# Routing the second experts batch by batch, and starting their blocks among the attention's last steps

## What is computed

```python
x = x + attn0(layernorm(x))                 # linear attention, width 64
x = x + ffn0(layernorm(x))                  # 8 experts, top 2, and a shared expert
x = x + attn1(layernorm(x))                 # 16 heads, window of 128 keys on each side
x = x + ffn1(layernorm(x))                  # 8 experts, top 1

def ffn1(x, W1, W2, Wg, bg):                # W1 (8, 256, 1024), W2 (8, 1024, 256)
    xf = x.reshape(4096, 256)
    one_hot = jax.nn.one_hot(jnp.argmax(xf @ Wg + bg, axis=-1), 8)
    h = jax.nn.gelu(jnp.einsum('td,edh->eth', xf, W1), approximate=True)
    return jnp.einsum('etd,te->td', jnp.einsum('eth,ehd->etd', h, W2), one_hot)
```

## Time and profile before

| | |
|---|---|
| median of 3 runs | 1568.0 us (1565.64 to 1570.33) |
| the profiled execution | 1571.8 us, its span 1568.9 us |
| TensorE busy | 1431.9 us, 91% of the span |
| VectorE, GpSimd, ScalarE busy | 740.2, 450.8, 449.9 us |
| mean granted TensorE clock | 0.954 of 2.4 GHz |
| bytes moved by DMA | 139.78 MB |

### The profile page before, as it was taken

The page is one execution under the profiler, slowest core; times in us unless marked ns, Lnnn a source line. Parts: engine busy times, 40 slices in busy tenths (PEclk is TensorE's granted clock), DMA queues, the critical chain, the costliest instruction groups (busy, mean ns, idle before and its releaser), DMA issues.

```text
span 1568.9 us, 23779 instructions
## 1 busy us (share of the span) xinstructions
PE 1431.9 (91%) x7707; PEld 1037.5 (66%) x7707; DVE 740.2 (47%) x2386; ACT 449.9 (29%) x763; POOL 450.8 (29%) x533
## 2 busy tenths in 40 slices
PE   7999999899999999897988989889887569999998
PEld 4666655567777776455555656666655359999997
DVE  5643347333333333336677777777662342222221
ACT  1211211011111121113455555565544111111121
POOL 1100000143222220603345354453222023443443
PEclk9998999999999999998899999999988779999999
DMA  9300100011122111134335354553430941111111
GB/s 336 102 28 27 41 0 1 14 51 61 61 64 63 63 62 44 57 97 143 90 110 164 120 149 119 154 157 100 120 105 15 338 162 51 51 55 49 50 56 32
DMA packets 88356, 139.78 MB, mean 89 GB/s; under 512 B 10637, under 2 KB 52751, under 8 KB 88240
## 3 DMA queue, kind: packets, MB, share of 16 engines
q1 hardware_dynamic: 72832, 104.02, 21.1%
q0 software_dynamic: 12096, 32.13, 7.1%
q10 hardware_dynamic: 3312, 2.12, 0.5%
HBM read 86.46 MB, written 52.17 MB: 88 GB/s over the span
## 4 chain that ended last, share of the span: by engine, by line
PE 76%; DVE 9%; DMA 6%; issue 4%; ACT 3%; POOL 1%; ACTq 1%; DVEq 0%; SPq 0%; POOLq 0%
PE psum L663 11%; PE psum L544 9%; PE psum L845 8%; PE psum L867 7%; PE psum L642 6%; PE psum L555 5%; PE psum L734 5%; PE psum L689 3%; DMA qT<-max_T 3%; PE psum L711 3%; DVE work L1519 2%; PE psum L471 2%; PE psum L790 2%; ACT arena L1045 2%; PE psum L461 2%
## 5 line engine op out<-in xcount | busy, mean ns | idle before, releaser
L1519 DVE CUSTOM_DVE_ANT_0 work<-psum,mask 128x384 bf16<-128x384 f32 (+1 forms) x512 | 229.7, 487 | 122.4 <-PE psum L689 119.4
L1045 ACT ACTIVATE arena<-psum 128x512 f32<-128x512 f32 (+1 forms) x256 | 179.5, 703 | 182.4 <-PE psum L711 172.9
L1626 POOL DMA_INDIRECT work<-normed,token_of x110 | 104.4, 949 | 395.7 <-PE psum L624 211.3
L663 PE MATMUL psum<-arena,work 128*128 x568 | 187.5, 473 | 2.8 <-ACT work L961 2.4
L689 PE MATMUL psum<-kz,qT 96*128 96x384 f32 (+1 forms) x512 | 170.2, 413 | 7.8 <-DVE small L1519 7.0
L711 PE MATMUL psum<-qT,kz 100*128 100x384 f32 (+1 forms) x512 | 131.5, 337 | 31.1 <-ACT arena L1045 16.8
L544 PE MATMUL psum<-arena 128*128 128x512 f32 x320 | 152.1, 621 | 0.0
L845 PE MATMUL psum<-work,X 128*128 128x128 f32 x1248 | 146.9, 276 | 0.0
L845 PEld LDWEIGHTS psum<-work,X 128*128 128x128 f32 x1248 | 143.8, 193 | 0.1
L689 PEld LDWEIGHTS psum<-kz,qT 96*128 96x128 f32 x512 | 91.1, 199 | 76.9 <-issue 38.9
L867 PE MATMUL psum<-arena,work 128*128 x624 | 141.0, 379 | 0.0
(11 more groups left out here) (170 smaller groups left out, 1987.7 us busy)
## 6 DMA issues: line engine op xcount, KB each, us to landing
strips<-hi SPq DMA_DIRECT2D x64, 256.0 KB
arena<-in_w SPq DMA_DIRECT2D x16, 1024.0 KB, 12.6
kz<-strips SPq DMA_DIRECT2D x64, 192.0 KB, 3.2
qT<-strips SPq DMA_DIRECT2D x32, 384.0 KB, 4.9
results<-work SPq DMA_DIRECT2D x71, 128.0 KB, 1.7
strips<-lo SPq DMA_DIRECT2D x32, 256.0 KB
normed<-work SPq DMA_DIRECT2D x15, 512.0 KB, 5.1
X<-in_x SPq DMA_DIRECT2D x8, 512.0 KB, 9.5
```

Source lines behind the costliest of these rows:

```text
L663: m = e.matmul(psum[:, pair[u], 0:INTER], xsT0[:, b % 2, c * P:(c + 1) * P], wu0[:, bass.ds(x, 1), c, u * INTER:(u + 1) * INTER], start=(c ...
L1045: e.activation(pT[:, j, 2 * half:2 * half + 2, 0:w], src, ACT.Exp, scale=1.0 / E ** 0.5).then_inc(p_exped, 1)
L1519: e.tensor_tensor_reduce(masked[:, n % 2, 0:w], psum[:, bank_of["scores", u, i, hd], at:at + w], mask[:, P - off:P - off + w], 1.0, MASKED ...
L1626: e.indirect_dma_start(out=xs[:, b % 3, :], out_offset=None, in_=normed[l], in_offset=bass.IndirectOffsetOnAxis(ap=token_of[:, l, b:b + 1] ...
```

## The change

Routing by batch. The gate of batch b comes at step 46 instead of 50. Then `dve_pick` (step 47) finds each token's expert, `pe_ranks` (48) counts with 8 small products each token's rank among all tokens of its expert so far, `dve_slots` (49) makes its place, and `pool_place` (50) writes the token numbers with four indirect transfers into a table in DRAM, in which each expert has 32 rows of 128 places. The table is filled with a padding number at step -12.

Two lists. After batch 4 (step 113) and after batch 7 (step 161) `dve_list` works out which rows of the table hold blocks, `pool_list` gathers them, `pe_list` and `dve_tokens` turn them into lists of tokens. The first list has the full blocks of the first five batches, 12 of them; the second has the other 27.

Blocks in the loop. `ROWS_AT`, `UP_AT` and `DOWN_AT` say in which step a block's transposes, first and second product stand: the 12 early ones from step 128 to 166, among the attention's last steps, the others one every two steps from 168. `FETCH_AT` says when its rows are gathered.

Weights. `sp_weights` loads the block's own w1 and w2 (1 MB each) from DRAM for every block, into two buffers each; the array in DRAM is laid out so that a partition's part is one run of 8 KB. VectorE's copies of w1 are gone, and so are TensorE's reads of the expert's number. The first products of all blocks now use PSUM banks 0 and 1, the transposes bank 2, the second products the ring of 6 and 7.

Batch 6's two stores to DRAM move from SyncE to ScalarE.

```diff
-TURN_AT, GATE_AT = (-11, 43), 50
+TURN_AT, GATE_AT = (-11, 43), 46
+EARLY_B = 5
+EARLY = (EARLY_B * N - NX * (P - 1)) // P
+LISTED_AT = (PRE * (EARLY_B - 1) + 49, PRE * (B - 1) + 49)
+ROWS_AT = [128, 129, 131, 133, 135, 137, 139, 141, 144, 149, 153, 159]
+UP_AT = ROWS_AT[1:] + [162]
+DOWN_AT = [132, 134, 136, 138, 140, 142, 145, 150, 154, 160, 163, 166]
+LATE_AT = LISTED_AT[1] + 7
+ROWS_AT += [LATE_AT - 1] + [LATE_AT + 2 * k for k in range(NBLK1 - EARLY - 1)]
+UP_AT += [LATE_AT + 2 * k for k in range(NBLK1 - EARLY)]
+DOWN_AT += [LATE_AT + 2 * k + 3 for k in range(NBLK1 - EARLY)]
+FETCH_AT = [122, 123, 124] + [at - 4 for at in ROWS_AT[3:EARLY]]
+FETCH_AT += [max(at - 4, LISTED_AT[1] + 5) for at in ROWS_AT[EARLY:]]
...
+            m = e.matmul(psum[:, bk, 0:n], before[:, :], flat, start=True, stop=False, skip_group_check=True)
+            for d in range(1, TPB):
+                m = e.matmul(psum[:, bk, d * w:n], ones[:, :], flat[:, 0:n - d * w], start=False, stop=False,
+                             skip_group_check=True)
+            e.wait_ge(so_far_made, b + 1)
+            for t in range(TPB):
+                m = e.matmul(psum[:, bk, t * w:(t + 1) * w], ones[:, :], so_far, start=False, stop=True,
+                             skip_group_check=True)
...
+        def pe_up1(e, k):
+
+            e.wait_ge(xsT_made[1], k + 1)
+            e.wait_ge(w1_got[k % 2], 16 * (k // 2 + 1))
+            for u in range(2):
+                fill(e, ("up1", k, u), u)
...
+                for k in blocks_at(s, ROWS_AT, 1):
+                    act_turned_rows(e, 1, k, xsT1)
+                for k in blocks_at(s, UP_AT, 1):
+                    act_hidden1(e, k)
                 for u, j in unit(s, 7, 4):
                     act_exp(e, u, j, 0)
...
-                        if (norm, b, i) == (3, B - 1, 1):
+                        if norm == 3 and b >= B - 2 and i == 1:
                             keep_residual(e, b)
                             keep_normed(e, 1, b)
...
                 for b, _ in batch(s, GATE_AT + 1):
-                    dve_gate(e, 1, b)
+                    dve_pick(e, b)
+                for b, _ in batch(s, GATE_AT + 3):
+                    dve_slots(e, b)
+                for i in range(2):
+                    if s == LISTED_AT[i]:
+                        dve_list(e, i)
...
+                for b, _ in batch(s, GATE_AT + 4):
+                    pool_place(e, b)
+                for i in range(2):
+                    if s == LISTED_AT[i] + 2:
+                        pool_list(e, i)
+                for k in blocks_at(s, FETCH_AT):
+                    pool_rows1(e, k)
+                for k in blocks_at(s, UP_AT):
+                    pool_residual1(e, k)
+                for k in blocks_at(s, DOWN_AT, 2):
+                    pool_out(e, k)
...
+            for t in range(b * TPB, (b + 1) * TPB):
+                e.indirect_dma_start(out=slots, out_offset=bass.IndirectOffsetOnAxis(ap=slot_of[:, 2, t:t + 1], axis=0),
+                                     in_=token_no[:, t:t + 1], in_offset=None).then_inc(placed, 16)
...
+            if k == 0:
+                e.wait_ge(*done["again", NU - 4, TPB - 1, G - 1])
+            if k == 1:
+                e.wait_ge(*done["again", NU - 3, TPB - 1, G - 1])
+                e.wait_ge(*done["again", NU - 2, TPB - 1, G - 1])
+            if k >= 2:
+                e.wait_ge(*done["up1", k - 2, 1])
+            x = e.value_load(blk_expert[0:1, 1, k:k + 1], min_val=0, max_val=NX - 1)
+            e.dma_start(w1_now[k % 2].rearrange("p c n -> p (c n)"),
+                        a["w1"][bass.ds(x, 1), :, :].rearrange("x p n -> p (x n)")).then_inc(w1_got[k % 2], 16)
+            if k >= 2:
+                e.wait_ge(*done["down1", k - 2])
+            e.dma_start(w2_now[k % 2].rearrange("p c n -> p (c n)"),
+                        a["w2"][bass.ds(x, 1), :, :].rearrange("x p n -> p (x n)")).then_inc(w2_got[k % 2], 16)
...
+            for k in range(NBLK1):
+                sp_weights(e, k)
```

580 lines of the change are left out of this document (322 added, 258 removed).

## The result

The changed kernel takes 1694.6 us (median of 4 runs, 1690.0 to 1698.8), the kernel before 1566.8 beside it: a ratio of **1.082** (95% interval 1.077 to 1.086). The prediction said 1559, in a range of 1538 to 1578. The profiled execution has a span of 1688.1 us, 119.2 more than the 1568.9 of before. Every further kernel was timed beside runs of its own of the kernel before, whose medians lie between 1561.1 and 1567.1 us; so a difference between two medians can hold up to 6 us that are not the edit's, and the ratios are the safer measure.

A forecast was written before the change was run, and what follows sets the result against it. TensorE was taken as the bound, its stretch from 1188 to 1282 us as the target. Terms -60 + 19.4 + 6.7 + 15 + 10 = -8.9 us took the 1568.0 median to 1559, range 1538 to 1578.

The forecast's parts named there:

- Routing taken out of the gap: Stretch from last maxima to late blocks: waits, low clock and routing work, plus row waits, could go; ceiling 60 us.
- Picks and ranks: Attention, batches 0 to 4: new TensorE products 10.4 us plus 9 us behind VectorE, 19.4 us slower.
- The gate moves from step 50 to 46, same work: nothing by itself.: Attention, each batch's gate: standing four steps earlier is the same work and costs 0 us.
- GpSimd's four scatters ... nothing.: Attention, each batch: four issues of 1.31 us ahead of the next mask, which has about 8 us to spare; cost 0.
- Waits from step 128 on: Early blocks among the attention's last steps: remaining TensorE waits and low clock cost 15 us, bounds 9 and 25.
- (4) of "What would show it": ScalarE behind step 128: seven table loads of 1.28 us, with exponentials' waits next to them.
- The stream: 27 late blocks: loading weights for every block adds 0.37 us a block, 10 us in all.
- L: Late blocks: time from a second product's end until two 1 MB weight transfers land; 7.7 to 8.7 us, 8.2 taken.
- the rival: Late blocks' first products waiting for w1: weight loading becomes the bound, L 9.5 us, kernel 1576 us; chance 0.18.
- sign (5): Late blocks' weight transfers: w1 lands near 6 us.
- its rivals: Late blocks bound by weight loading, 1576 us, chance 0.18; attention paying 30 us for the new steps, 1570 us, chance 0.15.

The follow-up runs named there:

- SyncE's order: The changed kernel with SyncE issuing block k's first matrix before block k - 1's second, and expert numbers read ahead of the waits: 1643.9 us, ratio 1.049.
- gate_46: The kernel before with only the second gate's step moved from 50 to 46: 1590.9 us, ratio 1.017.

## Why the prediction was wrong, step by step

The attention's 94.1 us, by differences of first to last maxima, are: picks and ranks 500.4 - 479.9 = **20.5**; the gate's place 529.7 - 500.4 = **29.3**; scatters 574.0 - 529.7 = **44.3**, of which 26.7 go with the table's spacing (17.9 of them come back at 32 KB) and 17.6 stay, among them 9.0 of wait for the first list and 6.1 for the masks behind the long products of VectorE (L725's waits between first and last maxima, 9.9 against 3.8). Each term comes from one execution and holds for this order of taking away.

*Routing taken out of the gap, -60.* The first part of the reasoning stands: this time is waits, and once the causes were mended the end did get shorter.

*Picks and ranks, 19.4.* 20.5: right, as closely as one execution can tell. The smallest of the three terms was the one worked out best.

*"The gate moves from step 50 to 46, same work: nothing by itself."* **Wrong: 22 us in the kernel before, 29 in the changed one.** The work is the same, the bank is not. The step saw the ring of two banks and charged it for ranks; it did not ask who holds the bank at step 46. The output rows do, until VectorE has copied them. And it took a wait at its length: of the 3.9 us lost in a batch, 1.5 were longer waits and 2.4 products at the lower clock behind them. Of the 22 and 29, 1.8 are batch 5's gate, which the prediction rightly had ahead of step 128.

*"GpSimd's four scatters ... nothing."* **Wrong: 44 us in the attention and up to 19 behind it, most of these the second list's wait (18.9 us, gone without the scatters).** Two sentences failed. The mask had time, but what stood next to it in GpSimd's queue, the bias addition, slid beside VectorE's small product. And the price of a scatter was taken from a gather's row, its issue on GpSimd, while nothing in the trace of before showed its landing. What the trace didn't show was not bounded from both sides: the list's wait was given the 2.8 us of a gather; it took 13.9 for the scatters, beside the weights, and 5.5 for the list. The Trainium skill (DMA: Bandwidth & Descriptors, Specifications) says that below 512 bytes the engine reads, modifies and writes; here 512-byte packets cost nothing and 4-byte ones 13 us in the same kernel, which agrees as far as the price goes; the reading back no run shows. Had the prediction weighed that rule, the scatters would have been a rival.

*Waits from step 128 on, 15.* TensorE waits 39.1 us from there to the first late rows: 18.9 for the second list (forecast 1.5), 5.8 for an early block's rows (forecast none), the rest about as forecast. The exponentials wait 4.4 us for all four, where 1.9 as now and 4.9 behind Gelus were forecast. The table loads are seven, four for Gelus and three for exponentials, as (4) of "What would show it" has it. The prediction left open whether a drain of 1.38 us comes with each. ScalarE's timeline of the changed kernel decides it, where Gelu, load and exponential stand without a wait:

```profile
1297.71 1.02 ACT L1139 ACTIVATE arena<-psum 128x1024 f32<-128x1024 f32 x1 [2.77 <-PE psum L870]
1298.75 1.28 ACT L1105 ACT_TABLE_LOAD   x1
1300.04 1.08 ACT L1105 ACTIVATE arena<-psum 128x512 f32<-128x512 f32 x2
```

The Gelu ends at 1298.73 and the exponential starts at 1300.04, 1.31 us later: the load and no drain.

*The stream, 10.* The mechanism was right, and the size of L was off. From the end of the second product (1584.5) to w1's landing (1594.0) L is 9.5 us, the rival's number, and (7.02 + 9.5)/2 = 8.26 us; the 24 pitches measured are 8.34 on average. This is one pair of a scattered lot: w1 lands 6.0 to 9.4 us after its issue in the late blocks, with a median of 8.0, where sign (5) had 6. So 27 blocks cost **30 us** and not 10. The 1.3 us by which L was short are two terms: w1's issue comes 1.11 us behind w2's, since the register is read between them (forecast 0.4; the rival names it, with no price), and w1 then takes 8.4 us where 8.2 - 0.4 = 7.8 were left for it. With all else as forecast this alone would have made the kernel 11 us slower than before.

*Sum.* -8.9 became +119.2 by the spans, 128 us off: 29 + 44 from two steps at "nothing", 17 of the list, 20 of the stream, 6 of the rows, 1 of the ranks are 117; the 11 left lie among the early blocks and in the clock of that stretch (0.88), and were not taken apart, but that SyncE's order gave back 6.0 there. The chance of slower was 0.20, and its rivals put slower on the stream or on ranks. The two largest losses had no rival, since the prediction had closed them with a word.

## What to carry to other kernels

"Same work, moved" has a price of its own: before writing nothing, read from the order which bank, port and queue entry stands next to the new place, and count a wait of TensorE with the slow products behind it. Don't price a scatter by its issue or by a gather: small writes to DRAM need their own landing time, and if the places written at once lie 16 or 32 KB apart, try another distance: half a kilobyte more took 27 us off the attention here. With streamed weights, let each buffer's reload be issued by the event that frees it, with its address read ahead: a half block saved there made 8.3 us a block into 7.24.

## What the runs showed of the hardware

- 512 writes of 4 bytes to eight places 16 KB apart landed 8.9 to 11.4 us after the last issue in the attention, and other transfers 8 us behind them ran at 60 to 75 GB/s with the DMA engines fully busy. At 32 KB they took 12.4 us, at 16.5 KB 5.8 to 6.9. Beside weight transfers of 1 MB they took 11.9 to 13.9 us at any of these distances, and in the changed kernel the transfers took 13.3 to 17.4. The Trainium skill (DMA: Bandwidth & Descriptors, Latency and other measured facts) reports a loss of rate at row pitches that are large powers of two, from 512 KB up, as an inference about channels of the memory; these runs show a loss at 16 and 32 KB for small writes that 512 bytes more took away in part. Whether the cause is the same, no run shows.
- A product of 4 columns on VectorE took 2.20 us instead of 0.17 beside a GpSimd addition of 2.38 and ended 0.04 us behind the next GpSimd instruction.
- A switch of ScalarE's table between a Gelu and an exponential took 1.31 us from the end of one to the start of the other, a load of 1.28 with nothing else.
- In gate_46, a wait of 1.75 us and, 2.8 us on, one of 0.88 were followed by a granted clock of 0.50 (1.2 GHz) in a stretch that had been at 1.00, and nearly doubled a product of 1.02 us. A single wait of 1.18 us at this place in the kernel before left the clock at 1.00.
